# Second attention: q and k turned once a batch and stacked through a DRAM scratch

## What is computed

```python
qkv = jnp.einsum('bld,ed->ble', x, w_qkv)
qkv = qkv.reshape(B, L, 3, H, D).transpose(2, 0, 3, 1, 4)   # H = 16 heads of D = 16
q = rmsnorm(q, q_norm_w)
k = rmsnorm(k, k_norm_w)
scores = jnp.einsum('bhqd,bhkd->bhqk', q, k) * D ** (-0.5)
attn = jax.nn.softmax(scores, axis=-1)
out = jnp.einsum('bhqk,bhkd->bhqd', attn, v)
...
return jnp.einsum('bld,ed->ble', out, w_proj) + b_proj
```

## Time and profile before

| | us |
|---|---|
| median of three runs (1408.67 to 1409.96) | 1408.72 |
| the profiled execution | 1408.91 |
| its span | 1407.1 |
| PE busy in the span | 1368.9 (97%) |
| PE's weight loads | 1221.1 (87%) |
| DVE | 920.9 (65%) |
| ACT | 820.0 (58%) |
| POOL | 761.9 (54%) |

### The profile page before, as it was taken

How to read it: one execution, slowest core, us unless ns; L and a number is a source line. 1 busy time by engine, 2 the same in 40 slices (tenths; PEclk the granted TensorE clock), 3 DMA queues, 4 the chain that set the end, 5 groups by cost and what they waited for, 6 DMA issues and landing times. The chain is left out here.

```text
span 1407.1 us, 25856 instructions
## 1 busy us (share of the span) xinstructions
PE 1368.9 (97%) x8950; PEld 1221.1 (87%) x8950; DVE 920.9 (65%) x1793; ACT 820.0 (58%) x2172; POOL 761.9 (54%) x757
## 2 busy tenths in 40 slices
PE   9999899999999999999999999899999999999997
PEld 7887798999899989998999888788889888889887
DVE  6655566565656565656665665677777878777764
ACT  5553444554544555445544544378787788778873
POOL 2651433454434454435544443477669677777764
PEclk9999999999999999999999999999999999999999
DMA  5995333334332343223433334144233242342442
GB/s 197 323 330 198 85 91 89 92 80 120 100 94 52 101 130 99 75 75 98 114 86 94 113 75 165 68 122 150 83 98 123 68 150 84 120 120 92 143 122 90
DMA packets 85681, 165.64 MB, mean 118 GB/s; under 512 B 16720, under 2 KB 27664, under 8 KB 83248
## 3 DMA queue, kind: packets, MB, share of 16 engines
q1 hardware_dynamic: 85552, 163.99, 38.3%
HBM read 99.90 MB, written 22.09 MB: 87 GB/s over the span
## 5 line engine op out<-in xcount | busy, mean ns | idle before, releaser
L775 POOL TENSOR_TENSOR a_pr<-a_pr,a_ri 128x512 f32<-128x512 f32 x128 | 133.5, 1043 | 299.1 <-DVE a_ri L955 299.1
L832 ACT ACTIVATE a_pr<-a_score,a_nb 128x256 f32<-128x256 f32 x256 | 119.3, 471 | 266.3 <-DVE a_nb L947 266.3
L1337 POOL TENSOR_TENSOR l_pr<-l_pr,l_ri 128x512 f32<-128x512 f32 x128 | 133.5, 1043 | 119.0 <-DVE l_ri L1714 118.1
L1465 ACT ACTIVATE l_pr<-l_score,l_nb 128x256 f32<-128x256 f32 x256 | 119.2, 472 | 80.8 <-DVE l_nb L1680 80.2
L58 PE MATMUL a_job<-s_xs,s_wh 128*128 128x512 f32 x384 | 153.9, 401 | 1.0 <-PEq L221 1.0
L60 PE MATMUL a_job<-s_xs,s_wl 128*128 128x512 f32 x384 | 151.7, 395 | 0.0
L59 PE MATMUL a_job<-s_xs,s_wh 128*128 128x512 f32 x384 | 151.3, 394 | 0.0
L947 DVE TENSOR_REDUCE a_nb<-a_score 128x2 f32<-128x512 f32 x128 | 88.5, 692 | 85.0 <-PE a_score L1026 83.3
L1680 DVE TENSOR_REDUCE l_nb<-l_score 128x2 f32<-128x512 f32 x128 | 87.5, 684 | 34.0 <-PE l_score L1820 33.4
L960 DVE TENSOR_TENSOR a_pt<-a_turn,a_pt 128x512 fp32r<-128x512 f32 x128 | 87.5, 683 | 24.2 <-ACT a_pt L840 24.2
L1844 PE MATMUL l_out<-s_wh,l_vp 128*128 128x256 f32 x512 | 91.6, 300 | 0.9 <-DVE s_wh L1684 0.9
(11 more groups left out here) (257 smaller groups left out, 4780.3 us busy)
## 6 DMA issues: line engine op xcount, KB each, us to landing
s_wl<-wgu_scratch SPq DMA_DIRECT2D x56, 512.0 KB, 4.8
a_sk<-a_rotk SPq DMA_DIRECT2D x384, 64.0 KB, 2.0
a_sq<-a_rotq SPq DMA_DIRECT2D x256, 64.0 KB, 2.0
s_xs<-xn_scratch SPq DMA_DIRECT2D x14, 1024.0 KB, 5.6
l_wd<-wd_scratch SPq DMA_DIRECT2D x56, 256.0 KB, 2.7
a_raw<-in_w SPq DMA_DIRECT2D x30, 256.0 KB, 3.0
wgu_scratch<-f_split SPq DMA_DIRECT2D x14, 512.0 KB, 4.7
f_praw<-in_moe_w SPq DMA_DIRECT2D x14, 384.0 KB, 4.5
```

Of the source, the lines that this page charges most:

```text
L775: pool.tensor_tensor(e, e, ri[:, n % 2, :].unsqueeze(2).broadcast_to([P, 2, SEQ]), ALU.mult)\
L832: i = act.activation(pr[:, n % 2, t, :], PS[n % 2][:, t * SEQ:(t + 1) * SEQ], ACT.Exp, bias=nb[:, n % 2, t:t + 1], accum_out=sm[:, n % 2, ...
L1337: pool.tensor_tensor(e, e, ri[:, n % 3, :].unsqueeze(2).broadcast_to([P, 2, SEQ]), ALU.mult)\
L1465: i = act.activation(pr[:, n % 3, t, :], PS[n % NPS][:, t * SEQ:(t + 1) * SEQ], ACT.Exp, bias=nb[:, n % 3, t:t + 1], accum_out=sm[:, n % 3 ...
```

## The change

The rows of q and k are no longer split and duplicated in SBUF. Once they are weighed, two jobs a batch, `X0` and `X1` (one for each half of 8 heads), turn them on PE as they are, four transposes of 128x128 each. ACT copies the high halves to `tqk` and DVE writes the low ones. SP stores `tqk` to two scratch tensors in DRAM (four stores of 128 KB a half), and loads from there, for two pairs of heads at a time, both parts of `zq` and the stack `sk`, with the duplicates made by the source's access pattern. The rings `zq` and `sk` hold four pairs. The scores wait for the landing of the loads. The columns of `w_qkv` and the norm's weights are put in another order (`head_columns`), so the sums of squares and the scaling walk with a stride of four. SP's program calls the new transfers, by the slot at which they are due, ahead of the transfer of a tile that waits for something of that slot or a later one. The planner's goals change from 30.6 and 14 to 28.7 and 18.

```diff
-    NJ, NPS, NSTK, NGU, ND, NCB, NHID = 3, 1, 3, 3, 3, 3, 3
+    NJ, NPS, NSTK, NGU, ND, NCB, NHID = 3, 1, 4, 3, 3, 3, 3
+    PER_LOAD = 2
-    UNIT, SLOT_GOAL, EARLY_GOAL = 10, 30.6, 14
+    UNIT, SLOT_GOAL, EARLY_GOAL = 10, 28.7, 18
+
+    def X_AT(m):
+        return (8, 9) if m == 0 else (8, 10)
...
-        m, r = divmod(n + 4, H1)
-        if r % 2 == 0 and 0 <= m < BATCH:
-            jobs.append((f"S{r // 2}", m))
+        if b + 1 < BATCH and u in X_AT(b + 1):
+            jobs.append((f"X{X_AT(b + 1).index(u)}", b + 1))
...
-        stq, stk = n_.sb("stq", [P, TB, H1, 4, D1]), n_.sb("stk", [P, TB, H1, 4, D1])
-        zq, sk = n_.sb("zq", [P, NSTK, 2, SEQ], F32R), n_.sb("sk", [P, NSTK, SEQ], F32R, shift=OFF)
+        tqk = n_.sb("tqk", [P, 2, 2, 2, SEQ], F32R)
+        zq, sk = n_.sb("zq", [P, 2, NSTK, SEQ], F32R), n_.sb("sk", [P, NSTK, SEQ], F32R, shift=OFF)
...
+                def store_stack(m, half):
+                    wait_free(sp, (f"X{half}", m))
+                    for low in range(2):
+                        sp.dma_start(qs_dram[m % 2, half, :, :, low].rearrange("h d p n -> (h d) p n"), tqk[:, half, 0, low, :].bitcast(F32))                           .then_inc(tqk_out[half], 16)
+                        sp.dma_start(ks_dram[m % 2, half, :, low].rearrange("h d p n -> h (d p) n"), tqk[:, half, 1, low, :].bitcast(F32))                           .then_inc(tqk_out[half], 16)
+
+                def load_stack(i):
+                    pair = i * PER_LOAD
+                    m, p = divmod(pair, H1 // 2)
+                    at = slice(pair % NSTK, pair % NSTK + PER_LOAD)
+                    if p % 4 == 0:
+                        sp.wait_ge(tqk_out[p // 4], 16 * 4 * (m + 1))
+                    if pair >= NSTK:
+                        sp.wait_ge(S["score_full"], 2 * (pair + PER_LOAD - NSTK))
+                    half, j = divmod(p, 4)
+                    for h in range(2):
+                        own = qs_dram[m % 2, half, h, :, :, j:j + PER_LOAD].rearrange("d c p n -> (d c) (p n)")
+                        sp.dma_start(zq[64 * h:64 * h + 64, h, at, :].bitcast(F32).rearrange("r p n -> r (p n)"),
+                                      own.unsqueeze(0).broadcast_to([2, 2 * D1, PER_LOAD * SEQ])).then_inc(zq_in[stack_of(i)], 16)
+                    own = ks_dram[m % 2, half, :, :, :, j:j + PER_LOAD].rearrange("h c d p n -> (h c d) (p n)")
+                    sp.dma_start(sk[:, at, :].bitcast(F32).rearrange("r p n -> r (p n)"),
+                                  own.unsqueeze(1).broadcast_to([4 * D1, 2, PER_LOAD * SEQ])).then_inc(sk_in[stack_of(i)], 16)
+
+                def transfers(n):
+                    m, u = n // H1 + 1, n % H1
+                    if m < BATCH and u - 1 in X_AT(m):
+                        store_stack(m, X_AT(m).index(u - 1))
+                    if n % (2 * PER_LOAD) == 0 and 0 <= n // (2 * PER_LOAD) + 1 < N // (2 * PER_LOAD):
+                        load_stack(n // (2 * PER_LOAD) + 1)
...
+                def stack_until(n):
+                    while due[0] <= n:
+                        transfers(due[0])
+                        due[0] += 1
+
                 for K in range(L + 1):
                     if 2 <= K < L:
+                        stack_until(AT["U", K - NGU] if K >= NGU else SLOTS[0])
                         load_gu(K)
                     if K >= 1:
+                        stack_until(AT["D1", K - 1 - ND] if K > ND else SLOTS[0])
                         load_d(K - 1)
                     s, k = step_of(K)
                     if k == NSH + 1 and s < NSTEP:
+                        stack_until(AT["C", s])
                         store_combine(s)
...
-                        for h in range(2):
-                            act.activation(zq[64 * h:64 * h + 64, r, h, :], bank[64 * h:64 * h + 64, 0:SEQ], ACT.Copy)
-                        act.activation(sk[:, r, :], bank[:, SEQ:2 * SEQ], ACT.Copy).then_inc(free_of(item), 1)
+                    elif name[0] == "X":
+                        half = int(name[1])
                         wait_full(act, item)
+                        if m >= 1:
+                            act.wait_ge(tqk_out[half], 16 * 4 * m)
+                        act.activation(tqk[:, half, :, 0, :], bank[:, :].rearrange("p (r n) -> p r n", r=2), ACT.Copy).then_inc(S["turned_hi"], 1)
...
+                    elif name[0] == "X":
+                        half = int(name[1])
+                        dve.wait_ge(S["turned_hi"], 2 * m + half + 1)
+                        dve.tensor_tensor(tqk[:, half, :, 1, :], bank[:, :].rearrange("p (r n) -> p r n", r=2),
+                                          tqk[:, half, :, 0, :], ALU.subtract).then_inc(free_of(item), 1)
...
-                    if u % 2 == 0:
-                        wait_free(pe, (f"S{u // 2}", m))
+                    if u % (2 * PER_LOAD) == 0:
+                        i = n // (2 * PER_LOAD)
+                        pe.wait_ge(zq_in[stack_of(i)], 16 * 2 * (n // (2 * NSTK) + 1))
+                        pe.wait_ge(sk_in[stack_of(i)], 16 * (n // (2 * NSTK) + 1))
```

More of the change, by code:

```diff
@@ L1196, in stage_layer1 @@
         gu_in = l1.gu_in
+        zq_in, sk_in = ([n_.sem(f"{s}_in{i}") for i in range(NSTK // PER_LOAD)] for s in ("zq", "sk"))
+        tqk_out = [n_.sem(f"tqk_out{i}") for i in range(2)]
         d_in, cb_in = ([n_.sem(f"{s}_in{i}") for i in range(3)] for s in ("d", "cb"))
@@ L1223, in tokens @@
             return slice(at, at + P)
-        def heads(t, part, half):
-            at = part * D + half * P
-            return qk[:, t, at:at + P].rearrange("p (h d) -> p h d", d=D1).unsqueeze(2).broadcast_to([P, 8, 2, D1])
-        def half_of(rows, t, half):
-            return rows[:, t, 8 * half:8 * half + 8]
         def wait_merged(engine, s):
@@ L1442, in job_out @@
                             act.activation(gt[:, m % 2, :], bank[:, :], ACT.Tanh, scale=0.5).then_inc(S["tanh_ready"], 1)
-                def k_hi(m, half):
-                    act.wait_ge(S["scaled"], m + 1)
-                    if m >= 1:
-                        wait_full(act, (f"S{4 * half + 3}", m - 1))
-                    for t in range(TB):
-                        act.activation(half_of(stk, t, half)[:, :, 0:2, :].bitcast(F32R), heads(t, 1, half), ACT.Copy)\
-                           .then_inc(S["k_hi"], 1)
-                def q_hi(m, half):
-                    act.wait_ge(S["weighted"], m + 1)
-                    if m >= 1:
-                        wait_full(act, (f"S{4 * half + 3}", m - 1))
-                    for t in range(TB):
-                        act.activation(half_of(stq, t, half)[:, :, 0::2, :].bitcast(F32R), heads(t, 0, half), ACT.Copy)\
-                           .then_inc(S["q_hi"], 1)
                 def exps(n):
@@ L1766, in do_item @@
                                             [w[:, q, c, 2 * D:3 * D] for q in range(2)], c == 0, c == KC - 1)
-                    elif name[0] == "S":
-                        p = int(name[1])
-                        pe.wait_ge(S["q_lo"], 4 * m + 2 * (p // 4) + 2)
-                        pe.wait_ge(S["k_lo"], 4 * m + 2 * (p // 4) + 2)
-                        for k, rows in enumerate((stq, stk)):
+                    elif name[0] == "X":
+                        half = int(name[1])
+                        pe.wait_ge(S["weighted"], m + 1)
+                        for part in range(2):
                             for t in range(TB):
-                                i = pe.transpose(bank[:, k * SEQ + t * P:k * SEQ + (t + 1) * P],
-                                                 rows[:, t, 2 * p:2 * p + 2, :, :].rearrange("p h r d -> p (h r d)"), ident[:, :])
+                                at = part * D + half * P
+                                i = pe.transpose(bank[:, part * SEQ + t * P:part * SEQ + (t + 1) * P], qk[:, t, at:at + P], ident[:, :])
                     elif name[0] == "P":
@@ L1884, in program @@
             stage_attention0(nc, a, sh, s0, l1, xn0, g0, w1, wp, wgu)
-        stage_layer1(nc, sh, l1, wgu, wd, ct, out)
+        stage_layer1(nc, sh, l1, wgu, wd, ct, qs, ks, out)
 def tile_weights(gate, up, down):
@@ L1896, in tile_weights, with head_columns @@
     return np.stack(tiles)
+def head_columns(w):
+    import numpy as np
+    qk = w[0:2 * D].reshape(2, 2, 4, 2, D1, D).transpose(0, 1, 3, 4, 2, 5).reshape(2 * D, D)
+    return np.concatenate([qk, w[2 * D:]])
 def proj_rows(w):
```

54 lines of the change are left out of this document (18 added, 36 removed).

## The result

The changed kernel takes **1499.49 us**, median of 4 runs (1496.89 to 1501.43); the kernel before, beside it, 1409.34 (1408.67 to 1411.87). The ratio is **1.0635**, 95% interval 1.061 to 1.066. The direction was forecast, the size wasn't: 1453 was predicted, 1381 to 1468 the range.

A forecast was written before the change was run, and what follows sets the result against it. The prediction took PE's own work to bound the last stage. From 1408.9: −21.1 transposes, −5 waits relieved, +1 moved work, +13 start, +56 batch changes = 1453 us, range 1381 to 1468.

The forecast's parts named there:

- transposes taken from PE: Last stage: 192 fewer transposes at 0.11 us each, all on the path that sets the end, −21.1 us.
- strided sum: DVE's sum of squares, read in another stride: nothing to twice its some 1.2 us a batch more, covered by idle time.
- other engines relieved, work moved, new transfers if spread: Last stage: −5 us from shorter PE waits, +1 from MoE work put ahead of first scores; spread transfers unnoticed.
- two engines, start and batch changes: q loads and k stores run on two DMA engines: +13 us at the start, +56 at seven batch changes.
- What bounds the kernel: Last stage: PE's own work sets the pace; it really waits little, an estimated 17 us lost.
- fourth case: Rival: transfers on sixteen engines, but DVE and POOL late in shorter slots, PE's waits growing 9 us; 1398 us, chance 0.05.
- The relief of 5 us: PE's waits ahead of the turns: 5 of 17 us go as ACT, DVE and POOL lose work; bounds −10 to +6.
- the 56 that were forecast for the changes of batch: Scores wait for late loads at seven batch changes, 8 us each (4 to 12): +56 us, range +28 to +84.
- The start: Eight stores hold two engines ahead of the first loads, so first scores come at 938 instead of 925: +13 us.
- The base of 925: First scores without two-engine delay: 918.5 plus 5.6 of moved work and about 1 for an X job, 925 us.
- Sixteen engines, 1384: Rival: new transfers spread like today's, so both two-engine terms go; 1384 us (1376 to 1395), chance 0.32.
- Two engines, hidden: Rival: SP runs further ahead, leaving only the two engines' capacity and the start as cost; about 1430 us, chance 0.13.

The follow-up runs named there:

- spread_all: Changed kernel, same bytes, each q load cut into its two copies and k rows stored once per head, so no transfer has two rows outermost: 1412.2 us.
- before_turns: Kernel before with one transpose instead of four in each S job (turning q and k rows), 192 left out, everything else kept: 1403.9 us.
- spread_squares: spread_all with ACT writing the squares in the order DVE sums them, so the sum reads without a stride: 1405.3 us.
- no_wait: Changed kernel, all transfers kept, but the scores read a stack of zeros never loaded, so PE waits for none of the new transfers: 1483.6 us.
- no_cb: Changed kernel, all transfers kept, but POOL multiplies by a resident tile of ones instead of cb and doesn't wait for it: 1498.3 us.
- spread_loads: Changed kernel with only the q loads cut into their two copies, k stores still with two heads outermost: 1452.4 us.
- spread_stores: Changed kernel with only the k stores changed, one per head with 64 rows outermost, q loads still with two copies outermost: 1443.2 us.
- spread_early: spread_all with the first load of zq and sk issued ahead of the store of the routing weights: 1412.2 us.
- actq_after: Changed kernel with its 160 new transfers issued by ACT near the start of each slot instead of by SP, shapes unchanged: 1513.2 us.
- spread_old_goals: spread_all with the planner's goals of the kernel before, 30.6 and 14 instead of 28.7 and 18: 1432.5 us.

## Why the prediction was right or wrong

The error of 46.5 us parts as follows, each line by differences of the medians above. The price of the transposes comes from the kernel before and that of the stride from spread_all, so that they simply add up is assumed.

| step | forecast | measured | by |
|---|---|---|---|
| transposes taken from PE | −21.1 | −5.4 | before_turns less before |
| strided sum (forecast: sum and scaling) | 0 | +6.9 | spread_all less spread_squares |
| other engines relieved, work moved, new transfers if spread | −4 | +1.5 | what is left of +3.0 |
| two engines, start and batch changes | +69 | +87.3 | changed less spread_all |
| sum | +44 | +90 | |

**What bounds the kernel: wrong in part.** "PE's own work sets the pace" is the step whose mechanism failed: 21.1 us of transposes were counted in full and were worth 5.4, which is 15.7 of the error. I read 97% busy and an idle of 28.6 us as an engine with work that counts in full. But the turns already waited for DVE in 14 places and for POOL in 9, which says that in those slots the other engines end at about the same time as PE. Take work from PE there, and it waits. My fourth case, sixteen engines with slots too short, at 1398 us, had this mechanism, and it had 0.05.

**The other engines.** The counts and the durations of single instructions were right, and DVE and POOL come out near what was reckoned (DVE is busy 911 us instead of 921, POOL 737 instead of 762). ACT is relieved of 71 us and not of 90; presumably copies that follow each other overlap, as the chain gives 0.26 us to one of 375 ns. The strided sum "between nothing and twice" was within its bounds as a duration (2.01 us for 1.21), but "which its idle time covers" was wrong: DVE's idle is elsewhere in the slot. The relief of 5 us didn't come: the waits ahead of the turns grew, 38.9 us of PE's idle in spread_all against 28.6.

**Two engines: right in what is short, wrong in who waits.** The count of small packets and the first cb at 929.68 are as predicted, and so is the chain at the change to batch 5 (counted from 0): from the burst ahead, whose wd is issued at 1245.36, to the landing of sk at 1282.19 it takes 36.8 us, where 36.5 was worked out. But at the first heads of batches 1 to 7 the scores wait 3.2, 5.2, 2.1, 8.2, 1.9, 8.7 and 2.4 us, 31.7 in all, and only three of these lie in the forecast 4 to 12. Not foreseen was that cb and the gate/up weights in the same queue stop other engines just as long (no_wait, no_cb); the term took the scores for the only ones. The waits that PE has in front of its turns for DVE and POOL are 68 us, 46 in spread_all.

**Their size: the term of 69 measured 87.3, 18 us more, and the rows lay this on the clock.** PE's work from the first scores to the last is the same in the changed kernel and in spread_all. The stretches (length, then busy PE, PEld, DVE, ACT, POOL; clock, DMA share, GB/s), first the changed kernel, then spread_all:

```profile
945.20:1477.70 532.50, 450.53 (x2928) 399.84 (x2929) 338.45 (x724) 290.74 (x825) 316.42 (x387) 0.94 0.45 140
930.10:1387.90 457.80, 430.56 (x2927) 384.01 (x2928) 339.26 (x724) 288.03 (x825) 316.45 (x387) 0.99 0.57 166
```

The changed kernel takes 74.7 us longer: PE is idle for 82.0 us instead of 27.2, 54.7 more, and the same matmuls keep it busy for 20.0 us more. The 54.7 come near the 56 that were forecast for the changes of batch, but in part by luck, as the waits stand elsewhere. The 20.0 had no term in the prediction. The chain at the change to batch 5 shows what they are (start, us, what):

```profile
1269.79 12.40 DMA l_sk<-ks_scratch
...
1282.33 0.77 PE l_score L1827 x2
...
1284.38 0.43 PE l_job L58
...
1288.20 0.23 PE l_job L58
```

PE stood idle for 5.9 us, did one slot's turns and products, and waited 1.9 us more for sk. After that a product takes 0.43 us instead of 0.23, for some five microseconds. The stretches around it (busy PE and PEld, then DVE, ACT, POOL; the granted clock is the third number from the end):

```profile
1276.00:1282.00 6.00, 1.94 (x8) 1.67 (x8) 3.95 (x11) 2.81 (x8) 2.54 (x3) 0.57 0.40 126
1282.00:1284.00 2.00, 1.67 (x8) 1.70 (x9) 0.87 (x2) 0.14 (x1) 0.41 (x1) 0.50 0.12 48
1284.00:1286.00 2.00, 2.00 (x7) 1.61 (x7) 0.59 (x2) 1.52 (x5) 2.00 (x5) 0.50 0.20 28
...
1288.00:1290.00 2.00, 2.00 (x13) 1.75 (x13) 1.93 (x6) 1.18 (x6) 0.29 (x1) 1.00 0.84 306
```

The clock stands at 0.50, the lower of its two levels (1.2 GHz), from within the wait until after 1286, and PE works through it. In stretches of 2 us from 944 to 1478 I added PE's busy time times the missing share of the clock: 21.8 us in the changed kernel, 14.6 in spread_loads, 9.6 in spread_stores, 3.6 in spread_all, none before. The difference to spread_all, 18.2, is nearly all of the 20.0. No experiment held the clock up with the waits left in, so this is reckoned from rows, not shown apart. At this change PE works 4.6 us at the lower clock behind the wait for sk, which is 2.3 us lost on top of it; the changed kernel has twelve places with a lowered clock between 944 and 1428, of unequal length.

**The start: 15.1 us by spread_all, 13 forecast.** The base of 925 was wrong: even spread, the first scores start at 930.1, since SP takes from 912.1 to 923.9 to come to sk through eight stores and eight further issues, about half a microsecond each (2.1 us of it is the landing of the ct store), and an issue had been reckoned at nothing. spread_early bears this out: with the first load issued earlier they start at 926.3. On two engines the first scores came at 945.2, not 938: 15.5 us behind the first cb, where 8.5 had been reckoned.

**The rivals.** "Sixteen engines, 1384" is what spread_all builds, and that takes 1412: its condition, the spread, holds there, and its sum doesn't, since the transposes were worth 5.4 us and the strided sum cost 6.9. "Two engines, hidden", about 1430, fell: the landings of sk came too late at the start and at every change of batch.

## What to carry to other kernels

Before a broadcast or a split by head is put in front of a transfer's pattern, count its outermost dimension on both sides; two there made one transfer slow and, through the common queue, every other transfer late. A high busy share doesn't make an engine's every microsecond count: look at how close the others come in at the waits it has, or take the work out alone and measure, as before_turns did for 21 us that were worth 5. And a wait that is removed shows only what stands behind it; remove the candidates in pairs.

## What the hardware showed

- Issuing a transfer can hold up the engine that issues it: SP took 0.50 to 0.73 us for a store at the start, 3.31 for the one at 917.13 and 7.58 for the sk load at 939.33, and ACT stood idle for 68 us when it issued the same transfers (actq_after).
- A sum over 128x1024 in fp32 takes DVE 2.01 us with a stride of four elements and 1.21 without; ACT's 128x512 squares, read from PSUM, take 0.60 us in either order; DVE's scaling of 128x1024 became quicker by the reordering, 1.30 us instead of 1.56.
- Leaving transposes out of the kernel before didn't touch its clock (0.999). In the changed kernel PE's clock fell at waits, 7.8 us of them at the change to batch 5; in spread_old_goals it also stayed at its lower level, 0.50, from 1384.0 to 1411.8 us, where PE was busy for 18.6 of 27.8 us and waited 1.47 us at a time.
